# ScalarE makes the exponentials of a unit ahead of the copy of turned probabilities

## The chip, the cores and the metric

The kernel runs on one core of one Trainium2 chip. The metric is the device time of one launch in microseconds. Three runs of the kernel before took 4431.72 us in the median (4425.48 to 4433.78).

## The reference

The reference is one layer of a vision transformer over 64 images of 3 x 224 x 224, in fp32. It makes 196 patch tokens an image, adds two class tokens (198 tokens of width 192), applies attention and then a mixture of experts, each with a residual. The attention is what matters here:

```python
q, k, v = (qkv[0], qkv[1], qkv[2])                       # 12 heads of 64
attn = jnp.einsum('bhqd,bhkd->bhqk', q, k) * scale
attn = attn + jnp.einsum('bhqd,qkd->bhqk', q, r_p_k) * scale   # relative positions
attn = jax.nn.softmax(attn, axis=-1)
out = jnp.einsum('bhqk,bhkd->bhqd', attn, v)
out = out + jnp.einsum('bhqk,qkd->bhqd', attn, r_p_v)
out = out.transpose(0, 2, 1, 3).reshape(b, n, QKV_DIM)
return out @ proj_w.T + proj_b
```

## The kernel before

Three stages run one after the other: tokens (to about 465 us), attention (to about 3461 us), experts. The attention stage takes the images in 8 groups of 8. In a group there are 6 pairs of heads, and in a pair 16 units: one image and one head each, so 96 units (STEPS) in a group and 768 in all. A unit has 198 queries and 198 keys; both are handled in halves of 99.

Every engine runs through the same 96 steps of a group, and its instructions are written out in a fixed order. Semaphores tie the engines together. In step n:

- TensorE makes the scores of unit n (L1077), then turns the probabilities of unit n - 2 (four transposes, L1043) into one PSUM bank, the only one of its kind, then multiplies the turned probabilities of unit n - 3 with the values (L1060), and then does the step's jobs. Before it turns, it waits until POOL has normalised unit n - 2 and until ScalarE has copied the turned probabilities of unit n - 3 out of the bank (`probT_made`).
- VectorE takes the maxima of the scores (L870), inverts the sums of the unit before (L862), copies out the product of unit n - 3 (`put_out`, L854 and L855) and does its jobs.
- ScalarE copies the turned probabilities of unit n - 2 from PSUM (`turned_out`, L712), makes the exponentials of unit n (two ACTIVATEs at L724 with their sums) and does its jobs. The exponentials wait for the maxima (`peaks`), and for `turned`, since they write the buffer of probabilities that TensorE is turning (buffer i % 2).
- POOL multiplies the probabilities of a unit by the inverted sums (L631).

The jobs are the rest of the work, spread over the steps by a planner with a table of costs (`spread`): "first" jobs make queries (j below 4, copied by ScalarE at L686 to L689), keys (L692, L693), position terms (L697 on ScalarE, L814 on VectorE) and values (L703) of the next pair of heads; "last" jobs end the pair before (L822, L831 and L841 on VectorE, L1031 on TensorE). "turn" jobs make the normalised tokens of the next group: TensorE turns them (L991, L992), ScalarE copies them (L681, L682), VectorE makes the low part (L799, L800) and normalises the next ones (L780), and TensorE's projections (L998) need them. They lie at the end of a group. TensorE hands its results to the others through a ring of four PSUM banks. In two of the pairs of a group (p = 1 and p = 3) the planner's list has two query jobs behind each other, `f(K[0], Q[0], K[1], Q[1], Q[2], ...)`.

Once in each of the first seven groups, after step 72, ScalarE makes a square root for the next group's normalisation (L670, `deviation`). Square root and exponential lie in different tables, so an ACT_TABLE_LOAD stands before the square root and another before the next exponential.

Of the kernel before, what the change touches and what calls it, by code (L numbers as in the profile page):

```python
# [359 lines left out]
def attention_stage(nc, hidden0, qkv_w, proj_w, proj_b, tab_kv, tab_kh, tab_vv, tab_vh, hidden1):  # L360
# [16 lines left out]
    with ExitStack() as ctx:  # L377
# [152 lines left out]
        def base_of(g, v):  # L530

            return OPEN if v == "first" else g * G_JOBS + (OPEN + FIRST_JOBS - G_JOBS)
# [14 lines left out]
        with nc.Block() as block:  # L547
# [97 lines left out]
            def _(act):  # L645
                first = RAW // 2
# [22 lines left out]
                def deviation():  # L669
                    nc.scalar.activation(sd[:, :, :], mv[:, :, 1:2], ACT.Sqrt, bias=eps[0:HALF, :]).then_inc(sd_made, 1)  # L670
# [37 lines left out]
                def turned_out(n, i):  # L708
                    act.wait_ge(turned, n - 2 + 1)
                    if not isinstance(n, int) or n >= 4:  # L710
                        act.wait_ge(outs, n - 3)
                    nc.scalar.activation(probT[:, i % 2, :], t_bank[0:HALF, 0:2 * NTOK], ACT.Copy).then_inc(probT_made, 1)  # L712

                def group(g, s, v):
                    base = base_of(g, v)
                    for i in range(STEPS):
                        n = g * STEPS + i
                        if v != "first" or i >= 2:
                            turned_out(n, i)
                        act.wait_ge(peaks, n + 1)  # L720
                        if v != "first" or i >= 2:
                            act.wait_ge(turned, n - 1)
                        for h in range(2):
                            ins = nc.scalar.activation(prob[:, i % 2, h, :], s_bank[i % 2][0:HALF, h * NTOK:(h + 1) * NTOK],  # L724
                                                       ACT.Exp, bias=npeak[:, i % 2, h:h + 1],
                                                       accum_out=total[:, i % 2, h:h + 1])
                        ins.then_inc(exps, 1)
                        for j in spreads[v][i]:
                            job(base, g, v, *j)
                        if i == DEVIATION and v != "last":  # L730
                            act.wait_ge(mv_made, g + 2)
                            deviation()
# [10 lines left out]
                for j in opening[TURN:]:  # L743
                    job(0, 0, "opening", *j)
                groups(act, group)
                for i in range(STEPS, STEPS + 2):
                    turned_out((GROUPS - 1) * STEPS + i, i)
# [829 lines left out]
```

## Time and profile before

| what | value |
|---|---|
| median of three runs | 4431.72 us |
| the profiled execution | 4426.74 us |
| its span | 4425.0 us |
| mean granted TensorE clock | 0.963 |
| busy: TensorE, VectorE, ScalarE, POOL | 92%, 66%, 57%, 29% |
| copies of turned probabilities (L712) | 768 of 501 ns |
| exponentials (L724) | 1536 of 425 ns, and 1536 reads of their sums of 204 ns |

Busy time is the time in which an engine works on an instruction. An engine's idle time is put down to the instruction that ended it and to the engine that released that instruction. Successive instructions of ScalarE overlap: the next one can start before the row's time of the one before is over.

### The profile page before, as it was taken

To read this page: it belongs to the slowest core of one execution; us is meant where nothing else is said; L and a number is where in the kernel's file an instruction comes from. 1 tells how busy PE (TensorE), PEld (TensorE's weight loads), DVE (VectorE), ACT (ScalarE), POOL (GpSimd) and SP (SyncE) were. 2 spreads that over 40 slices of the span, in tenths; PEclk is the share of its full clock that TensorE was granted. 3 is DMA by queue.
4 is the path that set the end of the run, shared out by engine and by line. 5 is a ranking of instruction groups with operands and counts; after the bars stand their busy time and mean duration, and the time that the engine had idled before them with its cause. 6 is when DMAs were issued, how large, how long until landed. Compare 5 with 4: busy or idle time off the path is not lost. (4 is left out here: it accounts for less than half of the span.)

```text
span 4425.0 us, 84814 instructions
## 1 busy us (share of the span) xinstructions
PE 4084.1 (92%) x28203; PEld 3987.8 (90%) x28203; DVE 2922.1 (66%) x7468; ACT 2506.7 (57%) x6685; POOL 1273.7 (29%) x1423
## 2 busy tenths in 40 slices
PE   4986799899999999989989999999999799999999
PEld 4885699899899999989989998998999699999999
DVE  4675666666666766666666666666666577777776
ACT  2553666566666666656666666666665344444443
POOL 1232322222232222213222222221322244444443
PEclk8997899999999999999999999999999799999999
DMA  8543000000000000000000000000000222222222
GB/s 184 131 109 73 7 1 1 1 24 1 1 23 1 1 2 23 1 1 23 1 1 19 7 1 2 23 1 1 12 1 1 66 90 89 89 89 89 89 89 87
DMA packets 88973, 161.67 MB, mean 37 GB/s; under 512 B 5705, under 2 KB 75936, under 8 KB 85054
## 3 DMA queue, kind: packets, MB, share of 16 engines
q1 hardware_dynamic: 85118, 152.66, 12.1%
q0 software_dynamic: 944, 2.42, 0.3%
q8 instruction: 182, 2.98, 0.3%
q10 hardware_dynamic: 2576, 2.36, 0.2%
q14 instruction: 153, 1.25, 0.1%
HBM read 127.82 MB, written 29.60 MB: 36 GB/s over the span
## 5 line engine op out<-in xcount | busy, mean ns | idle before, releaser
L631 POOL TENSOR_TENSOR att_prob<-att_prob,att_total 99x396 f32<-99x396 f32 x768 | 650.9, 848 | 2279.0 <-DVE att_total L862 2279.0
L712 ACT ACTIVATE att_probT<-att_t 99x396 f32<-99x396 f32 x768 | 385.0, 501 | 737.4 <-PE att_t L1043 732.0
L870 DVE TENSOR_REDUCE att_npeak<-att_s 99x2 f32<-99x396 f32 x768 | 435.4, 567 | 451.7 <-PE att_s L1077 437.2
L724 ACT ACTIVATE att_prob<-att_s,att_npeak 99x198 f32<-99x198 f32 x1536 | 638.0, 425 | 80.3 <-DVE att_npeak L870 77.5
L1077 PE MATMUL att_s<-att_kx,att_qx 96*99 96x198 f32 (+1 forms) x3072 | 661.9, 339 | 4.5 <-DVE att_xres L841 2.3
L1060 PE MATMUL att_o<-att_probT,att_vx 99*96 99x198 f32 (+1 forms) x3072 | 663.1, 339 | 1.1 <-DVE att_rx L855 1.1
L1257 POOL TENSOR_TENSOR ffn_hidden<-ffn_relu 128x384 f32<-128x384 f32 x462 | 419.7, 914 | 494.8 <-ACT ffn_relu L1286 492.7
L1077 PEld LDWEIGHTS att_s<-att_kx,att_qx 96*99 96x99 f32 (+1 forms) x3072 | 494.3, 170 | 16.3 <-issue 5.3
L1286 ACT ACTIVATE ffn_relu<-ffn_h 128x384 f32<-128x384 f32 x462 | 226.3, 490 | 477.3 <-PE ffn_h L1503 476.5
L1515 PE MATMUL ffn_y<-ffn_down,ffn_hidden 128*128 128x192 f32 x2772 | 487.5, 326 | 0.0
L1060 PEld LDWEIGHTS att_o<-att_probT,att_vx 99*96 99x96 f32 (+1 forms) x3072 | 477.2, 181 | 5.8 <-issue 1.4
L1515 PEld LDWEIGHTS ffn_y<-ffn_down,ffn_hidden 128*128 128x128 f32 x2772 | 457.8, 190 | 1.2 <-issue 0.2
L854 DVE COPY att_oT<-att_o 64x198 f32<-64x198 f32 x768 | 277.1, 361 | 240.7 <-PE att_o L1060 233.2
L1043 PEld LDWEIGHTS att_t<-att_ident,att_prob 99*99 99x99 f32 x3072 | 396.1, 170 | 37.5 <-issue 21.9
L1043 PE MATMUL att_t<-att_ident,att_prob 99*99 99x99 f32 x3072 | 405.0, 255 | 20.3 <-ACT att_probT L712 16.5
L855 DVE COPY att_rx<-att_o 32x198 f32<-32x198 f32 x768 | 404.1, 526 | 10.4
L1408 DVE TENSOR_TENSOR ffn_hidden<-ffn_hidden,ffn_gates 64x384 f32<-64x384 f32 (+1 forms) x528 | 362.4, 702 | 20.5 <-issue 3.8
L1031 PE MATMUL att_p<-att_pw,att_oT 128*99 128x192 f32 x1536 | 292.6, 334 | 80.9 <-DVE att_oT L831 80.9
L1031 PEld LDWEIGHTS att_p<-att_pw,att_oT 128*99 128x99 f32 x1536 | 247.7, 169 | 89.6 <-issue 88.1
L724 ACT ACTIVATION_READ_ACCUMULATOR att_prob<-att_s,att_npeak 99x1 f32 x1536 | 313.3, 204 | 0.0
L814 DVE TENSOR_TENSOR att_qx<-att_p,att_qx 32x448 f32<-32x448 f32 (+1 forms) x384 | 226.4, 590 | 63.7 <-PE att_p L1008 35.4
L348 PE MATMUL tok_y<-tok_w,tok_patchT 128*112 128x192 f32 x1344 | 249.6, 339 | 10.5 <-DVE tok_y L282 10.5
(237 smaller groups left out, 8170.7 us busy)
## 6 DMA issues: line engine op xcount, KB each, us to landing
ffn_gates<-gate_rows SPq DMA_DIRECT2D x66, 768.0 KB, 5.0
tok_pixels<-in_x SPq DMA_DIRECT2D x24, 1568.0 KB
ffn_hid<-hidden SPq DMA_DIRECT2D x35, 288.0 KB, 3.0
att_xres<-hidden SPq DMA_DIRECT2D x8, 1188.0 KB
hidden<-att_xres SPq DMA_DIRECT2D x8, 1188.0 KB
ffn_acc<-hidden SPq DMA_DIRECT2D x33, 288.0 KB, 2.9
out_hidden<-ffn_acc SPq DMA_DIRECT2D x33, 288.0 KB, 2.4
hidden<-tok_rows SPq DMA_DIRECT2D x7, 1176.0 KB
```

The source lines that it names most:

```text
L631: nc.gpsimd.tensor_tensor(prob[:, i % 2, :, :], prob[:, i % 2, :, :], view(total[:, i % 2, :], [[1, 2], [0, NTOK]]), ALU.mult).then_inc(pr ...
L712: nc.scalar.activation(probT[:, i % 2, :], t_bank[0:HALF, 0:2 * NTOK], ACT.Copy).then_inc(probT_made, 1)
L724: ins = nc.scalar.activation(prob[:, i % 2, h, :], s_bank[i % 2][0:HALF, h * NTOK:(h + 1) * NTOK], ACT.Exp, bias=npeak[:, i % 2, h:h + 1], ...
L855: nc.vector.tensor_copy(view(rx[ext:ext + 32, p % 2, :], [[GB, NTOK]], b), o_bank[ext:ext + 32, 0:NTOK]).then_inc(outs_used, 1)
L870: nc.vector.tensor_reduce(npeak[:, i % 2, :], s_bank[i % 2][0:HALF, 0:2 * NTOK].rearrange("p (h k) -> p h k", h=2), AX.X, ALU.max, negate= ...
L1031: ins = nc.tensor.matmul(bank[0:HALF, t * DIM:(t + 1) * DIM], oT[:, s, cols], pw[:, weights, :], start=True, stop=True)
L1043: ins = nc.tensor.transpose(t_bank[0:HALF, k * NTOK + h * HALF:k * NTOK + (h + 1) * HALF], prob[:, j % 2, h, k * HALF:(k + 1) * HALF], ide ...
L1060: ins = nc.tensor.matmul(o_bank[0:M, 0:NTOK], vx[:, 2 * b + k, p % 2, v0:v0 + M], probT[:, j % 2, k * NTOK:(k + 1) * NTOK], start=(k == 0) ...
L1077: ins = nc.tensor.matmul(s_bank[i % 2][0:HALF, h * NTOK:(h + 1) * NTOK], qx[0:K, p % 2, head, q0:q0 + HALF], kx[0:K, p % 2, head, b * NTOK ...
L1257: nc.gpsimd.tensor_tensor(hidden[0:rows, s, j, :], relu[0:rows, (n + 2 * s) % 4, :], relu[0:rows, (n + 2 * s) % 4, :], ALU.mult).then_inc( ...
L1408: ins = nc.vector.tensor_tensor(hidden[lo:hi, s, j, :], hidden[lo:hi, s, j, :], gates[lo:hi, s, e, :], ALU.mult)
L1515: ins = nc.tensor.matmul(y_bank[t][:, 0:DIM], hidden[:, s, j, t * 128:(t + 1) * 128], down[:, j, :], start=(n == 0), stop=(n == HT - 1))
```

## The change

In the loop over the steps ScalarE calls `turned_out` behind the two exponentials and no longer ahead of their waits. The waits of the exponentials stay as they are. The two calls behind the last group, and the other engines' programs, are unchanged.

```diff
@@ -715,8 +715,6 @@
                     base = base_of(g, v)
                     for i in range(STEPS):
                         n = g * STEPS + i
-                        if v != "first" or i >= 2:
-                            turned_out(n, i)
                         act.wait_ge(peaks, n + 1)
                         if v != "first" or i >= 2:
                             act.wait_ge(turned, n - 1)
@@ -725,6 +723,8 @@
                                                        ACT.Exp, bias=npeak[:, i % 2, h:h + 1],
                                                        accum_out=total[:, i % 2, h:h + 1])
                         ins.then_inc(exps, 1)
+                        if v != "first" or i >= 2:
+                            turned_out(n, i)
                         for j in spreads[v][i]:
                             job(base, g, v, *j)
                         if i == DEVIATION and v != "last":
```

## Rows read from the trace of the kernel before

**Rows 1.** The page, part 1: busy us (share of the span) xinstructions.
```profile
PE 4084.1 (92%) x28203; PEld 3987.8 (90%) x28203; DVE 2922.1 (66%) x7468; ACT 2506.7 (57%) x6685; POOL 1273.7 (29%) x1423
```

**Rows 2.** TensorE's waits, 560 to 3465 us: total us, times, longest us.
```profile
PE att_p L1031 <- DVE att_oT L831: 80.2, 47, 2.3
PE att_p L998 <- DVE att_x L800: 31.1, 7, 4.4
...
PE att_t L1043 <- ACT att_probT L712: 15.0, 16, 1.0
PE att_t L1043 <- POOL att_prob L631: 3.7, 5, 0.8
```

**Rows 3.** Groups by line: busy, mean ns of one | idle before, releaser.
```profile
L712 ACT ACTIVATE att_probT<-att_t 99x396 f32<-99x396 f32 x768 | 385.0, 501 | 737.4 <-PE att_t L1043 732.0
...
L724 ACT ACTIVATE att_prob<-att_s,att_npeak 99x198 f32<-99x198 f32 x1536 | 638.0, 425 | 80.3 <-DVE att_npeak L870 77.5
```

**Rows 4.** Timeline of one step: start us, duration us, engine, line, [idle before].
```profile
3413.38 0.51 PE L1043 MATMUL att_t<-att_ident,att_prob 99*99 99x99 f32 x4
3413.59 0.57 DVE L870 TENSOR_REDUCE att_npeak<-att_s 99x2 f32<-99x396 f32 x1
...
3413.93 0.50 ACT L712 ACTIVATE att_probT<-att_t 99x396 f32<-99x396 f32 x1 [1.68 <-PE att_t L1043]
...
3414.33 0.42 ACT L724 ACTIVATE att_prob<-att_s,att_npeak 99x198 f32<-99x198 f32 x1
...
3415.21 0.59 PE L1043 MATMUL att_t<-att_ident,att_prob 99*99 99x99 f32 x4
```

**Rows 5.** Timeline, 937 to 942 us, behind two query jobs.
```profile
937.33 0.50 ACT L712 ACTIVATE att_probT<-att_t 99x396 f32<-99x396 f32 x1
...
938.04 0.51 PE L1043 MATMUL att_t<-att_ident,att_prob 99*99 99x99 f32 x4
...
941.30 0.50 ACT L712 ACTIVATE att_probT<-att_t 99x396 f32<-99x396 f32 x1
...
941.95 0.56 PE L1043 MATMUL att_t<-att_ident,att_prob 99*99 99x99 f32 x4 [0.95 <-ACT att_probT L712]
```

**Rows 6.** Timeline, 1514 to 1525 us, behind the square root.
```profile
1514.95 0.50 ACT L712 ACTIVATE att_probT<-att_t 99x396 f32<-99x396 f32 x1
...
1515.47 1.28 ACT L724 ACT_TABLE_LOAD   x1
...
1516.11 0.51 PE L1043 MATMUL att_t<-att_ident,att_prob 99*99 99x99 f32 x4
...
1516.46 0.86 PE L1060 MATMUL att_o<-att_probT,att_vx 99*128 99x198 f32 x4
...
1516.77 0.43 ACT L724 ACTIVATE att_prob<-att_s,att_npeak 99x198 f32<-99x198 f32 x1
...
1517.92 0.37 DVE L854 COPY att_oT<-att_o 64x198 f32<-64x198 f32 x1
...
1524.32 0.86 PE L1031 MATMUL att_p<-att_pw,att_oT 128*99 128x192 f32 x4 [2.29 <-DVE att_oT L831]
```

**Rows 7.** Timeline, 1547 to 1550 us, at the next group's tokens.
```profile
1547.58 0.43 ACT L724 ACTIVATE att_prob<-att_s,att_npeak 99x198 f32<-99x198 f32 x1 [0.56 <-DVE att_npeak L870]
...
1548.40 0.33 ACT L681 ACTIVATE att_x0h<-att_p 128x198 fp32r<-128x198 f32 x1
...
1549.81 0.67 PE L998 MATMUL att_p<-att_x0h,att_w0h 128*128 128x396 f32 x1 [4.44 <-DVE att_x L800]
```

**Rows 8.** ScalarE's waits, 1530 to 1572 us.
```profile
ACT att_prob L724 <- DVE att_npeak L870: 5.3, 7, 1.5
```

**Rows 9.** VectorE's waits, 560 to 3465 us.
```profile
DVE att_oT L854 <- PE att_o L1060: 228.5, 554, 1.4
...
DVE att_total L862 <- ACT att_prob L724: 17.0, 23, 1.1
```

**Rows 10.** Windows: span, busy us of PE, PEld, DVE, ACT, POOL, PEclk, DMA share, GB/s.
```profile
1524.30:1527.90 3.60, 3.58 (x18) 3.50 (x19) 1.28 (x4) 1.32 (x5) 0.85 (x1) 0.72 0.00 0
```

## The prediction

> **What bounds the kernel now.** I read the page first: TensorE is busy 92% of the span, ScalarE 57%, so time comes only from TensorE's idle stretches and whatever fills them [rows 1]. The diff touches the attention stage only (768 units in 8 groups of 96, about 490 to 3461 us of the span, so 3.9 us a unit), so the next view is what TensorE waits for there: 47 waits for VectorE's adds (L831), 7 long ones where the next group's tokens are turned (L998 behind L800), and 16 waits of 15.0 us in all for the turned probabilities' copy (L712) [rows 2]. That copy is what the change moves back. ScalarE itself idles 737 us in front of that copy and 80 us in front of the exponentials [rows 3]. So its work is spare on average; the question is where it is not.
>
> **What the edit does to an ordinary step.** Of the two waits that now precede the exponentials, one is no wait for a new thing: the exponentials of unit n overwrite the probabilities that TensorE is just turning (buffer i % 2), and the code keeps its wait on `turned`. So they can't start before the transposes end, change or no change. An ordinary step shows the size of it [rows 4]: transposes end at 3413.38 + 0.51 = 3413.89, copy at 3413.93, exponentials at 3414.33; VectorE's reduction ends at 3413.59 + 0.57 = 3414.16. New order: exponentials at about 3414.20, only 0.13 us earlier. The pair holds ScalarE for 0.82 us (worked out from rows at place 3); the copy then starts at 3415.02 instead of 3413.93 and ends at 3415.52. A copy holds ScalarE 0.40 us before the next instruction starts [rows 4], and TensorE restarts 0.15 us after a copy that it waits for (941.30 + 0.50 = 941.80, restart 941.95 [rows 5]). So TensorE's next transposes could start at 3415.67. A step of this stage is 3.9 us on average, transposes to transposes, and here 3413.38 + 3.9 = 3417.3: the delay lies free in nearly every step. The gain lies free as well: POOL and VectorE get the exponentials 0.13 us earlier, and TensorE's waits for POOL are 3.7 us in all [rows 2]. No instruction, byte or DMA is added or removed; SP's and POOL's queues aren't passed.
>
> The rule by which I look for losses: the copy is late by the exponentials' 0.8 us where ScalarE comes late anyway (it no longer goes first), and by more where the maxima are late; a ScalarE job behind both is late by the copy's 0.40 us where the copy was formerly hidden in the wait for the maxima.
>
> **Place 1, the heads' projections (16 times).** Twice in each group two query jobs follow each other, and ScalarE falls behind. Its copy of 937.33 comes 2.3 us after the transposes; TensorE turns on at 938.04; the next copy is at 941.30 and TensorE has waited 0.95 us for it at 941.95 [rows 5]. New: the first copy starts at 937.33 + 0.82 = 938.15, ends 938.65, TensorE goes on at 938.80, 0.76 us late. That alone is then absorbed by the 0.95 us wait. But the second copy also starts 0.82 us later, at 942.12, and TensorE goes on at 942.77 instead of 941.95: 0.82 us. The pair of steps costs 0.82, not the sum. There is one such wait for each of the 16 counted [rows 2]. Nothing later swallows it: VectorE, who makes the later waits at L831, itself waits for TensorE in between (554 waits at L854 [rows 9]), so it moves along. 16 x 0.82 = 13.1 us. Bounds: 0 (all absorbed) and 16 x 1.58 = 25 (no absorption between the two); I take 13.1, as the rows in sequence give it.
>
> **Place 2, after the deviation (7 times).** ScalarE has taken a square root and must load the exponentials' table again, 1.28 us. Before, the copy (1514.95) came ahead of the load (1515.47) [rows 6]. New: load 1514.95 to 1516.23, exponentials to 1517.05, copy ends 1517.57, TensorE's transposes start at 1517.72 instead of 1516.11: 1.6 us. What is late next is VectorE: it needed the product of 1516.46 + 0.86 = 1517.32 but came to it only at 1517.92; 1.6 us later, at 1518.92, it is 1.0 us behind. VectorE then works without a pause up to the adds that TensorE waits for at 1524.32 (2.29 us wait [rows 6]), so 0.6 of the 1.6 us vanish in that wait and 1.0 remains. 7 x 1.0 = 7.0 us (bounds 0 and 11).
> On this the Trainium skill has a rule that speaks against the change: "ScalarE: Activation LUTs", section "What ACT_TABLE_LOAD costs", gives a switch of the table set 1283 ns for the load and about 1380 ns more for a drain, some 2.66 us. By it the moved load would weigh 1.38 us more, 7 x 1.4 = 10 us on top. The row shows a load of 1.28 us with the exponentials 0.02 us behind it (1515.47 + 1.28 = 1516.75, then 1516.77 [rows 6]), so the trace gives no such drain here and the sum goes without it.
>
> **Place 3, where the next group's tokens are turned (7 times).** Here the three engines hand each other work and TensorE is the one that waits. ScalarE has made its copy, waits 0.56 us for the maxima, makes the exponentials at 1547.58 and, 0.82 us later, copies the turned tokens at 1548.40; VectorE's subtraction L800 follows; TensorE, idle for 4.44 us, goes on at 1549.81 [rows 7]. VectorE was late with the maxima, so the copy had been free; now it stands between exponentials and tokens, and the whole chain is 0.40 us later. The stretch of 42 us has 7 such waits for the maxima [rows 8]. I followed each: behind five of them a query or token job lies on this chain (the first three add up to the restart at 1549.81, one leads to TensorE's next restart near 1559.5, one to that near 1568), 5 x 0.40 = 2.0; and once ScalarE, late at 1553.6, must now wait 0.2 us for maxima. 2.2 us a group, 7 x 2.2 = 15.4 us. Bounds: 0, and 7 x 7 x 0.40 = 20. An early loss of 0.4 us on TensorE's side of the same stretch is hidden by the 4.44 us wait.
>
> **Last group.** Five steps without jobs: TensorE's next transposes at 3415.67 instead of 3415.21, [rows 4], 0.45 us, then an estimated 0.2 us a step, since from there on VectorE, held up by 0.45 us with its maxima, passes part of it on: about 1.5 us.
>
> **Sum.** 13.1 + 7.0 + 15.4 + 1.5 = 37 us. The profiled execution took 4426.7 us (span 4425.0), 5.0 below the median 4431.7 of three: 4463.7 on its scale, 4468.7 on the median's. I say 4466.
>
> **The clock.** TensorE's granted clock falls to its lower level, 1.2 GHz, after some of its waits: after the 2.29 us wait that ended at 1524.32 [rows 6] the next 3.6 us are granted 0.72 [rows 10], so the fall costs 3.6 x 0.28 = 1.0 us. After the 0.95 us wait it didn't: those transposes take 0.56 us, the ones before 0.51 [rows 5]. The new waits, 0.8 to 1.4 us, lie nearer to this one. I count no fall.
>
> **Rivals**, from 4429, which lies between the two times as 4466 does.
> Clock: the lengthened waits at places 1 and 2 (23) pull it down each time: 23 x 1.0 = 23 us more, 4489. For it: place 1 has two waits of 0.8 and 1.0 us within 4 us. Against: the 0.95 us wait cost nothing.
> Absorption: TensorE's losses at places 1 and 2 disappear in the 80 us of waits for L831, as 0.6 of 1.6 us does after the deviation; places 3 and the end remain: 4429 + 17 = 4446. Against: VectorE waits for TensorE more often than the reverse.
> Faster: exponentials no longer behind the copy. VectorE's reciprocals waited 23 times, 17.0 us, for them [rows 9], most where ScalarE is late; each comes 0.40 us earlier, 9 us, and the 3.7 us of waits for POOL go: 4429 - 13 = 4416. It decides if these reciprocals stand at the head of VectorE's chain to TensorE, rather than ahead of a wait for TensorE's product as at L854. I see them ahead of that wait.
> Nothing: two operations trade places inside ScalarE's 737 us of idle time and the late steps are too few: 4429. For it are the ordinary steps; against it the 16 waits where the copy is already what TensorE lacks.
>
> **How the numbers follow.** Forecast 64% (its own range 4452 to 4480: each place by a third either way), clock 12%, absorption 12%, faster 6%, nothing 6%. The range, 4440 to 4498, leaves out the two last and takes in the clock case with a third more; a change under 0.2% (9 us) can't be told from none here. Faster 0.06, same 0.08 (nothing, and the low end of absorption), slower 0.86.
>
> **What would show it.** TensorE's waits for the copy (L712) go from 16 with 15.0 us to about 45 with some 45 us, 1.4 us at each table load; the wait for L800 from 4.4 to about 5.2 us; ScalarE's idle time moves from in front of the copy to in front of the exponentials; the load at L724 stands ahead of the copy. Busy times stay. It is wrong if TensorE's waits for L712 stay near 15 us, if those at L831 shrink by as much as L712's grow, or if the mean granted clock changes by over 0.005.

## The result, and the profile after

| | before | after |
|---|---|---|
| median (20 runs each) | 4432.16 us | 4441.33 us |
| lowest to highest | 4416.45 to 4439.62 us | 4435.71 to 4446.98 us |
| profiled execution, its span | 4426.74, 4425.0 us | 4446.40, 4444.7 us |
| mean granted clock in it | 0.963 | 0.964 |

The ratio is 1.0025, 95% interval 1.0017 to 1.0033: slower by about 9 to 11 us, where 37 were forecast. The profiled executions stand 20 us apart; the one of before lies 5 us below its median and the one of after 5 us above.

TensorE's waits of the profile after, 560 to 3480 us (total us, times, longest us); against [rows 2] the copy's go from 15.0 to 38.3 us, those at L831 fall by 3.7, those for L800 grow by 4.2, and the wait for POOL is as good as gone.

```profile
PE att_p L1031 <- DVE att_oT L831: 76.5, 47, 1.8
PE att_t L1043 <- ACT att_probT L712: 38.3, 52, 1.4
PE att_p L998 <- DVE att_x L800: 35.3, 7, 5.1
PE att_p L998 <- issue: 21.3, 14, 2.3
...
PE att_t L1043 <- POOL att_prob L631: 0.2, 1, 0.2
```

ScalarE's groups after (busy, mean ns of one, idle before). Its idle time has moved from in front of the copy [rows 3] to in front of the exponentials, now L722, as forecast.

```profile
L722 ACT ACTIVATE att_prob<-att_s,att_npeak 99x198 f32<-99x198 f32 x1536 | 640.6, 422 | 931.6 <-DVE att_npeak L870 869.5 <-PE att_t L1043 58.7
L712 ACT ACTIVATE att_probT<-att_t 99x396 f32<-99x396 f32 x768 | 382.6, 498 | 1.8 <-PE att_t L1043 1.8
```

The timeline at place 1, the steps of [rows 5]. ScalarE is late at 947.70 and makes exponentials; the copy follows 0.82 us later and TensorE waits 0.57, then 0.96 us.

```profile
947.70 0.43 ACT L722 ACTIVATE att_prob<-att_s,att_npeak 99x198 f32<-99x198 f32 x1
...
948.52 0.50 ACT L712 ACTIVATE att_probT<-att_t 99x396 f32<-99x396 f32 x1
...
949.16 0.56 PE L1043 MATMUL att_t<-att_ident,att_prob 99*99 99x99 f32 x4 [0.57 <-ACT att_probT L712]
...
953.13 0.56 PE L1043 MATMUL att_t<-att_ident,att_prob 99*99 99x99 f32 x4 [0.96 <-ACT att_probT L712]
```

The timeline at place 2, the steps of [rows 6]: load, exponentials, copy, then TensorE; the wait at L1031 that follows is 1.75 instead of 2.29 us.

```profile
1528.21 1.28 ACT L722 ACT_TABLE_LOAD   x1
1529.51 0.43 ACT L722 ACTIVATE att_prob<-att_s,att_npeak 99x198 f32<-99x198 f32 x1
...
1530.33 0.50 ACT L712 ACTIVATE att_probT<-att_t 99x396 f32<-99x396 f32 x1
...
1530.97 0.56 PE L1043 MATMUL att_t<-att_ident,att_prob 99*99 99x99 f32 x4 [1.42 <-ACT att_probT L712]
...
1538.68 0.86 PE L1031 MATMUL att_p<-att_pw,att_oT 128*99 128x192 f32 x4 [1.75 <-DVE att_oT L831]
```

The timeline at place 3, the steps of [rows 7]: from the exponentials at 1561.03 to the tokens at 1562.23 it is now 1.20 us instead of 0.82, and TensorE waits 5.05 instead of 4.44 us.

```profile
1561.03 0.43 ACT L722 ACTIVATE att_prob<-att_s,att_npeak 99x198 f32<-99x198 f32 x1 [1.09 <-DVE att_npeak L870]
...
1561.85 0.50 ACT L712 ACTIVATE att_probT<-att_t 99x396 f32<-99x396 f32 x1
1562.23 0.34 ACT L681 ACTIVATE att_x0h<-att_p 128x198 fp32r<-128x198 f32 x1
...
1563.64 0.67 PE L998 MATMUL att_p<-att_x0h,att_w0h 128*128 128x396 f32 x1 [5.05 <-DVE att_x L800]
```

The longest of the new waits for the copy lies ahead of the 560 us from which the waits above are counted, at step 3 of the first group; the same wait was 1.31 us before, at 517.65.

```profile
519.39 0.56 PE L1043 MATMUL att_t<-att_ident,att_prob 99*99 99x99 f32 x4 [2.12 <-ACT att_probT L712]
```

**Step by step.** The start of each unit's scores (L1077) in both profiles gives the length of each of the 768 steps. Of the 96 steps of a group, those listed differ, and steps 82 to 86, where both kinds of difference mix; the others agree to 0.05 us but for a few at the start of group 0 and where two groups meet. (Differences after minus before, us, by group 0 to 7. Step 19 is the one from the scores of unit 19 to those of unit 20. The starts are read to 0.01 us, so a difference can be off by 0.02.)

```
step 19        0.77  0.79  0.78  0.78  0.78  0.75  0.77  0.77
step 51        0.78  0.78  0.78  0.77  0.78  0.75  0.79  0.78
step 74        1.64  1.63  1.63  1.63  1.64  1.65  1.64   -
step 75       -0.55 -0.56 -0.54 -0.54 -0.55 -0.56 -0.57   -
step 79        0.42  0.41  0.41  0.40  0.41  0.41  0.41   -
step 81        0.74  0.72  0.73  0.74  0.75  0.73  0.75  0.33
steps 12, 13   0.29 -0.01  1.66  0.04 -1.68  0.03 -0.01 -1.68
steps 28, 29   1.67  0.00 -0.01  0.00 -1.66 -1.67 -1.66 -1.66
step 45        0.02 -1.66 -1.65  1.66  0.00  0.00  0.00  0.01
steps 60, 61   1.68  0.01  0.01  0.00 -1.65 -1.67  0.03 -1.66
step 76       -0.01 -1.66 -1.67  1.67  0.01  0.00  1.67  0.01
```

The upper rows are the three places, the same in each group. The lower ones are 0 or 1.66 us of either sign: something that comes or doesn't. The windows of step 60 show what it is (columns as in [rows 10]; 4 us from the end of a wait for L831 that is 1.56 us long each time). Before, groups 2 and 3:

```profile
1466.80:1470.80 4.00, 4.00 (x28) 3.95 (x29) 2.59 (x8) 1.32 (x5) 0.85 (x1) 1.00 0.02 4
1839.80:1843.80 4.00, 4.00 (x16) 3.70 (x17) 1.29 (x4) 0.50 (x2) 0.45 (x1) 0.57 0.00 0
```

After, the same groups:

```profile
1480.00:1484.00 4.00, 3.95 (x28) 3.93 (x29) 2.52 (x7) 1.31 (x5) 0.84 (x1) 1.00 0.00 0
1858.20:1862.20 4.00, 4.00 (x16) 3.66 (x17) 1.29 (x4) 0.77 (x4) 0.77 (x1) 0.57 0.00 0
```

The same 1.56 us wait is followed once by the full clock, 28 products in 4 us, once by a fall to 1.2 GHz, 0.57 and 16 products. A fall costs TensorE 1.66 us there. Behind the waits of 1.56 to 1.76 us at steps 12, 28, 44 and 60 there are 16 falls in before and 9 in after: 7 x 1.66 = 11.6 us given back. (A fall is counted for a wait when the granted clock goes down in it or in the 3 us behind it.)

**The clock in all executions.** Two profiles alone wouldn't show that the falls are fewer. But the mean granted clock is on record for 87 executions of the kernel before (0.960 to 0.965, mean 0.9626) and for 31 of the kernel after (0.964 to 0.967, mean 0.9657). The profiled executions of before had 0.963 and 0.964 (experiment 1), above their mean, those of after 0.964 and 0.965 (experiment 6), below theirs.

### The profile page after: what moved, and what is told of

Its sections match the earlier page's. It is cut to its first block and busy times, and to the rows that moved or that the text cites. A ratio compares the mean times of both kernels' runs of the same rounds, so it can differ in the third digit from the quotient of the medians.

```text
span 4444.7 us, 84808 instructions
## 1 busy us (share of the span) xinstructions
PE 4083.2 (92%) x28203; PEld 3982.7 (90%) x28203; DVE 2919.8 (66%) x7468; ACT 2482.2 (56%) x6685; POOL 1271.8 (29%) x1423
## 5 line engine op out<-in xcount | busy, mean ns | idle before, releaser
L722 ACT ACTIVATE att_prob<-att_s,att_npeak 99x198 f32<-99x198 f32 x1536 | 640.6, 422 | 931.6 <-DVE att_npeak L870 869.5
L1077 PE MATMUL att_s<-att_kx,att_qx 96*99 96x198 f32 (+1 forms) x3072 | 658.0, 337 | 4.8 <-DVE att_xres L841 2.7
L1077 PEld LDWEIGHTS att_s<-att_kx,att_qx 96*99 96x99 f32 (+1 forms) x3072 | 490.7, 169 | 15.7 <-issue 5.6
L712 ACT ACTIVATE att_probT<-att_t 99x396 f32<-99x396 f32 x768 | 382.6, 498 | 1.8 <-PE att_t L1043 1.8
L1031 PE MATMUL att_p<-att_pw,att_oT 128*99 128x192 f32 x1536 | 292.2, 333 | 77.2 <-DVE att_oT L831 77.2
L1031 PEld LDWEIGHTS att_p<-att_pw,att_oT 128*99 128x99 f32 x1536 | 248.6, 169 | 86.1 <-issue 84.4
L722 ACT ACTIVATION_READ_ACCUMULATOR att_prob<-att_s,att_npeak 99x1 f32 x1536 | 301.7, 196 | 0.0
L348 PE MATMUL tok_y<-tok_w,tok_patchT 128*112 128x192 f32 x1344 | 250.1, 339 | 11.6 <-DVE tok_y L282 11.6
```

Source lines behind the costliest of these rows:

```text
L1031: ins = nc.tensor.matmul(bank[0:HALF, t * DIM:(t + 1) * DIM], oT[:, s, cols], pw[:, weights, :], start=True, stop=True)
L1077: ins = nc.tensor.matmul(s_bank[i % 2][0:HALF, h * NTOK:(h + 1) * NTOK], qx[0:K, p % 2, head, q0:q0 + HALF], kx[0:K, p % 2, head, b * NTOK ...
```

## The experiments

Each kernel was compared with the kernel before on the same chip. The median of before differs a little from one comparison to the next (4430.41 us for experiments 1 to 4, 4428.03 for 5 to 8, 4432.62 for 9 to 12), so kernels of different comparisons are to be held against each other by their ratios.

**1. The kernel before against itself.** No edit.

> The kernel before, unchanged, against itself. It leaves nothing out. Theory 'lottery of the clock': the waits of 1.4 to 2.3 us for the adds at L831 and L800 lie at the edge of a fall of the granted clock, a fall costs 1.66 us, and how many there are (33 stretches at the low level in the attention stage of the profiled execution) differs from one execution to the next. Then this profile shows another number of low stretches, another pattern of them, and a span of the attention stage that differs from 2942.9 us (first to last scores) by 3 to 10 us, while steps with no fall take the same time to 0.1 us. Rival 'the profile of before was typical': the same stage to within 1 us, and the change costs its 18 us there in every execution. The medians agree within 0.1% under both.

Measured: 4430.42 us (11 runs), before 4430.41 (33), ratio 1.0000 (0.9989 to 1.0010). From first to last scores 2946.5 us, 2942.5 in the other profile. The two profiles of one kernel differ by plus or minus 1.66 us at steps 12 and 13, 28 and 29, 44 and 45, 60 and 61, and 76, by up to 2.4 us at 82 to 86, and nowhere else by more than 0.2 us beyond the first group's first 20 steps and one place where two groups meet. There are 32 stretches at the low clock in the attention stage, 33 in the other profile. Step 60 in this profile, groups 1 and 2, where the first profile had the full clock:

```profile
1098.40:1102.40 4.00, 4.00 (x16) 3.66 (x17) 1.29 (x4) 0.54 (x2) 0.48 (x1) 0.57 0.00 0
1473.90:1477.90 4.00, 4.00 (x16) 3.70 (x17) 1.29 (x4) 0.47 (x2) 0.42 (x1) 0.57 0.02 4
```

So falls come and go between executions of one kernel; single profiles can't be compared by span. Their number at the four steps is 18 here.

**2 to 5. Places undone one by one.** The kernel after with the old order in some steps:

```diff
+    COPY_FIRST = (73,)                 # 2: behind the square root
+    COPY_FIRST = (18, 19, 50, 51)      # 3: behind the query jobs
+    COPY_FIRST = tuple(range(78, 86))  # 4: the tokens
+    COPY_FIRST = (18, 19, 50, 51, 73, *range(78, 86))  # 5: all three
...
+                        if i in COPY_FIRST and (v != "first" or i >= 2):
+                            turned_out(n, i)
                         act.wait_ge(peaks, n + 1)
...
-                        if v != "first" or i >= 2:
+                        if i not in COPY_FIRST and (v != "first" or i >= 2):
                             turned_out(n, i)
```

> The kernel after, with the old order (copy first) in one step of 96, the one behind the square root (step 73). Theory 'places': TensorE's waits for the copy lose their 7 longest (1.4 us each, 38.3 us in 52 becomes about 28 in 45), the step of 1.64 us at 75 of each group and the -0.55 behind it vanish, the kernel is 7.6 us faster than after, that is 0 to 0.1% above before (4432 + 9 - 8 = 4433 to 4437). Rival 'absorbed': the 2.29 us wait for L831 that follows takes its 1.64 us back wholly, time as after (4441).

> The kernel after, with the old order in the four steps of 96 where ScalarE is behind with query jobs (18, 19, 50, 51). Theory 'places': the 16 losses of 0.78 us vanish (12.5 us): as before or faster, 4429 to 4433; TensorE's waits for the copy fall from 38.3 us in 52 to about 22 in 36. Rival 'absorbed later': time as after (4441), since the waits at L831 grow by as much.

> The kernel after, with the old order in the eight steps of 96 where the next group's tokens are turned (78 to 85). Theory 'places': the wait for L800 is 4.4 us again instead of 5.1, and 2.1 us a group vanish, 15 us in all if my sum was right: 4427. Rival, from the two profiles (2.1 us a group in groups 0 to 2, about 0 in groups 3 to 6, where both have long stretches at the low clock): 5 to 7 us, 4435. If this place costs nothing in the median, time as after.

> The kernel after, with the old order in all three places (13 of 96 steps: 18, 19, 50, 51, 73, 78 to 85), the new order in the other 83. Theory 'places': no wait for the copy is left but the 16 of 0.95 us that were there before; time as before, 4430, within 0.1%. Rival 'the new order is itself worth something in the ordinary steps', for which speaks that the rest of the stage was 7 to 16 us shorter with it in four profiles: 4418 to 4424. Rival 'it costs in the ordinary steps too': 4435 and more.

| kernel | median us (runs) | ratio to before (interval) | waits for the copy, us (times) | falls at steps 12, 28, 44, 60; at the L831 wait of step 75 | mean clock of all executions |
|---|---|---|---|---|---|
| after | 4441.33 (20) | 1.0025 (1.0017 to 1.0033) | 38.3 (52) | 9; 3 | 0.9657 |
| 2, table | 4438.35 (11) | 1.0015 (1.0005 to 1.0025) | 28.0 (45) | 10; 2 | 0.9652 |
| 3, late | 4435.69 (11) | 1.0011 (1.0002 to 1.0020) | 29.0 (37) | 10; 6 | 0.9635 |
| 4, tokens | 4432.53 (11) | 1.0008 (0.9999 to 1.0017) | 34.3 (40) | 7; 4 | 0.9665 |
| 5, all three | 4432.29 (11) | 1.0010 (1.0000 to 1.0020) | 14.9 (17) | 18; 2 | 0.9618 |

For the kernel before the last two columns are 16; 3 and, in experiment 1, 18; 0, and 0.9626.

Kernels 2 and 3 came out 1 and 3 us above what was expected, kernel 4 5.5 us above the theory's 4427 and 2.5 under the rival's 4435. Each place is confirmed by its waits: 10.3 us go with the table's, 9.3 with the queries' (16 were expected), the 5.05 us wait for L800 becomes 4.4 again in kernel 4. Their gains (by the ratios 4, 6 and 8 us, against 7.6, 12.4 and 14.3 us of direct delay) are hardly above the intervals' plus or minus 4 us. They don't behave as a sum: with all three undone the kernel is no better than with the third alone. The waits of kernel 5 are those of before [rows 2]:

```profile
PE att_p L1034 <- DVE att_oT L834: 80.4, 47, 2.3
PE att_p L1001 <- DVE att_x L803: 31.0, 7, 4.4
...
PE att_t L1046 <- ACT att_probT L713: 14.9, 17, 0.9
```

and so is its number of falls, 18, though 83 of its 96 steps have the new order. With one place undone they are 7 to 10.

**6. The kernel after once more.** No edit.

> The kernel after, unchanged, once more. The 8 steps named for each group are slower by the same amounts to 0.05 us (0.78, 0.78, 1.64 with -0.55 behind it, 0.41, 0.74), and the falls of the clock behind the waits of 1.56 to 1.76 us stand elsewhere and number about 9 again, not the 16 and 18 of the two profiles of before. If they number 16 or more, their smaller number was chance.

Measured: 4439.83 us (11 runs), before 4428.03 (27), ratio 1.0027 (1.0018 to 1.0036). Falls at the four steps: 9 again, 7 of them at the same step of the same group as in the first profile of after. Waits for the copy 38.0 us in 52, and the steps named are the same to 0.03 us. The smaller number isn't chance: the mean clock is 0.9656 in these 11 executions and 0.9629 in the 27 of before beside them. It goes with the delays: 16 and 18 falls without them, 18 in kernel 5, which has hardly any, 7 to 10 with two or three of the three places. Kernel 3, with 6 falls more at step 75 and a mean clock of 0.9635, lies nearest to before.

**7 and 8. The clock taken out of play.** TensorE makes products of no use (fillers) in its long waits, in the order before (7) and after (8):

```diff
+                def fill(k, base, count):
+                    pe.wait_ge(free[k % RING], base + k // RING + PRIMED)
+                    for _ in range(count):
+                        nc.tensor.matmul(p_bank[k % RING][:, 0:384], ident[:, :], view(ident[:, :], [[0, 3], [1, 128]]),
+                                         start=True, stop=True)
...
+                    if v != "opening" and kind == "first" and j < 4 and p == NEXT:
+                        fill(k, base, (0, 11, 3, 1)[j])
...
                     if kind == "last" and j == 8:
+                        fill(k, base, 3)
                         all_read(base, v, "last", p, 7, other)
```

> The kernel before, in which TensorE no longer sits idle in its long waits: ahead of the waits for L831 it makes 3 products of the identity with itself (N = 384) in the free bank that its own job overwrites, and where the tokens are turned 11, 3 and 1. Nothing is left out. Theory 'the clock decides': the 32 or 33 low stretches of the attention stage go to under 12, each 1.6 us, and the kernel gains 25 to 35 us: 4395 to 4407. Rival 'the products only take time': they delay the restarts, 47 times some tenths of a us, and nothing is gained: 4430 to 4445.

> The kernel after with the same fillers. Theory 'the order costs 28 us, and fewer falls of the clock give 10 to 18 of them back': with the falls gone in both kernels, this one is 22 to 28 us above f1 (12.4 for the heads' projections, 7.6 at the table load, 2 to 8 at the tokens): about 4425. Rival 'the order costs 9 us': f2 stands 9 us above f1.

Measured: 7, 4400.14 us (5 runs), ratio 0.9939 (0.9925 to 0.9952), no fall in the attention stage: 'the clock decides' (4395 to 4407) held, and the 5 executions lie within 4.2 us of each other, where those of the kernel before spread over 23. 8, 4433.95 us (11 runs), ratio 1.0012 (1.0003 to 1.0021), 4 falls (two behind the 1.42 us waits for the copy, one behind the 2.11 us wait for it at step 3, one at step 16 of the first group). Between them 33.8 us, where the plain kernels differ by 9 to 12. Step by step the losses of the plain kernels stand there again (0.77 us at 19 and 51, 1.63 less 0.53, 0.41), only step 81 loses 0.33 instead of 0.74. The waits for the copy are the ones we know, in 7 and then in 8:

```profile
PE att_t L1052 <- ACT att_probT L712: 14.4, 16, 0.9
```

```profile
PE att_t L1052 <- ACT att_probT L712: 46.5, 59, 1.4
```

The rival for 8 (9 us) is out, and my 22 to 28 was too low.

**9. Only the moment moved.** The kernel before, TensorE busy 0.87 us longer twice a group:

```diff
+                    if kind == "last" and p in (0, 2) and j == 2:
+                        for n in (3 * 128, 64):
+                            nc.tensor.matmul(bank[:, 0:n], ident[:, :], view(ident[:, :], [[0, max(n // 128, 1)], [1, min(n, 128)]]),
+                                             start=True, stop=True)
```

> The kernel before, old order, in which TensorE works 0.76 us more twice in a group (products of the identity, N = 384 and 64, in the bank of the job that follows, at the heads' pairs where the new order costs 0.78 us). Nothing is left out. Theory 'the moment decides': which of the waits of 1.6 us is followed by a fall depends on when they come, and a group of 372 us repeats the falls. Then this delay alone lowers the falls behind the waits at steps 12, 28, 44 and 60 from 16 to 18 to about 9, and gives back its own 12 us: 4425 to 4434. Rival 'the new order itself protects the clock': the falls stay at 16 to 18 and the kernel is 12 us slower, 4442.

Measured: 4436.82 us (11 runs), before 4432.62 (16), ratio 1.0004 (0.9992 to 1.0017). The steps 22 and 54 are longer by 0.87 us in all 8 groups, 13.9 us, and the kernel by 2 to 4 us. Falls at the four steps: 11, and 3 at step 75. Mean clock of its 11 executions 0.9647, of the 16 of before 0.9626. The waits themselves are those of before:

```profile
PE att_p L1035 <- DVE att_oT L831: 80.2, 47, 2.3
PE att_p L1002 <- DVE att_x L800: 31.0, 7, 4.4
...
PE att_t L1047 <- ACT att_probT L712: 14.3, 16, 0.9
```

A delay alone, the order untouched, lowers the falls and gives a part of itself back: 10 to 12 of the 13.9 us by the medians and the ratio, at least 6 by the interval. The rival (4442, the order itself protects the clock) is out: 12 us would be a ratio of 1.0027. The median came 3 us above my interval's upper end of 4434. The delay here is work of TensorE, in kernels 2 to 4 it is waiting; the falls are fewer with both.

**10 to 12. Fillers made to size, and the ordinary steps.** In 10 (order before) and 11 (order after) the counts are 2 ahead of L831's waits and 6, 2 and 0 at the tokens; 12 is kernel 5 with the fillers of 7.

```diff
-                        fill(k, base, (0, 11, 3, 1)[j])
+                        fill(k, base, (0, 6, 2, 0)[j])
...
-                        fill(k, base, 3)
+                        fill(k, base, 2)
```

> The kernel before with fillers made to size: one product of N = 384 took 0.65 us, so three of them (1.95 us) were longer than the waits of 1.5 to 1.76 us, and eleven (7.2 us) longer than 4.44. Now 2 ahead of L831's waits, and 6, 2 and 0 at the tokens. Theory: no falls still, and 0.1 to 0.25 us saved at 47 places and up to 1.6 us at 7: 4388 to 4396. Rival: the 0.3 to 1 us of idle time that comes back lets the clock fall again: 4400 to 4410.

> The kernel after with the fillers of g2. Theory 'the order costs its sum once the clock is out of play': 30 to 37 us above g2. Rival 'some of f2 minus f1 came from the oversized fillers': under 25 us.

> The kernel after with the old order in the three places (13 of 96 steps), and the first, oversized fillers of f1. Theory 'the ordinary steps are free': f1 plus the 3.2 us that the first group's start costs (steps 3 to 16), 4400 to 4405. Rival 'the new order costs or saves in the 83 other steps': off by more than 5 us from f1.

Measured: 10, 4384.66 us (4 runs), ratio 0.9891 (0.9875 to 0.9906), the fastest of all, 3 us under the 4388 to 4396 expected. 11, 4418.52 us (7 runs), 0.9969 (0.9957 to 0.9980): 33.9 us above 10, inside the 30 to 37. 12, 4402.43 us (5 runs), 0.9935 (0.9921 to 0.9949), inside the 4400 to 4405: 2.3 us above 7, the ratios equal to 0.0004, and step by step only the first group's steps 3 to 14 differ, by 1.2 us in all. So the other 83 steps are free, as the timeline had shown. The waits of 10, then of 11:

```profile
PE att_p L1007 <- issue: 20.5, 21, 1.4
PE att_p L1040 <- DVE att_oT L831: 19.5, 46, 1.0
...
PE att_t L1052 <- ACT att_probT L712: 14.8, 16, 0.9
PE att_t L1052 <- POOL att_prob L631: 6.0, 8, 0.8
```

```profile
PE att_t L1052 <- ACT att_probT L712: 47.0, 59, 1.4
PE att_p L1007 <- issue: 26.0, 21, 1.8
PE att_p L1040 <- DVE att_oT L831: 15.5, 46, 0.5
...
PE att_t L1052 <- POOL att_prob L631: 0.2, 1, 0.2
```

Falls in the attention stage are 5 and 4, none at the four steps; 4 of those of kernel 10 lie at step 85, behind a wait of 0.77 us for POOL.

## Why the prediction was right or wrong

**The sum of direct delays was right to 3 us.** The kernel became 9 to 12 us slower. That is far under the 37 forecast, and 4441.33 lies below the forecast's own 4452 to 4480; that it is just inside the wider 4440 to 4498 is luck, since that low end was made for losses absorbed in the waits at L831. The sum itself said 37 us; with all but a few of the falls gone the two orders differ by 33.8 and 33.9 us. Its terms, by the step table (and for steps 83 and 85 of place 3 by kernels 7 and 8):

| term | predicted us | measured us |
|---|---|---|
| place 1, 16 times | 13.1 (0.82 each) | 12.4 (0.78 each) |
| place 2, 7 times | 7.0 (1.6 less 0.6) | 7.6 (1.64 less 0.55) |
| place 3, 7 times | 15.4 (2.2 each) | 13.3 (0.41 + 0.74, and 0.38 + 0.37 in kernels 7 and 8) |
| last group | 1.5 | 1.0 |
| start of the first group | not seen | 1.2 (a fall behind the 2.12 us wait in it) |

Place 3 was over-sized by one link: the steps give 0.41, 0.74, 0.38 and 0.37 us where I had counted five times 0.40 and once 0.2. At the start of the stage ScalarE is late as well, in steps 3 to 14 of group 0 alone; I had read no row there. That nothing absorbs the delays at place 1, that 0.6 us vanish behind place 2, and that the ordinary steps cost nothing, held. So did the choice of the row over the page on the table load: behind the 1.28 us load at 1528.21 the exponentials start at 1529.51, 0.02 us later, so there is none of the 1380 ns drain that "ScalarE: Activation LUTs" of the Trainium skill adds in its section "What ACT_TABLE_LOAD costs".

**The step that failed is "The clock ... I count no fall".** I asked whether the new waits would bring falls, and they hardly do: none behind the 0.57 and 0.96 us waits at place 1, none in either profile of after behind the 1.42 us waits at the table load, one behind the 2.12 us wait of step 3, where I had read no row. I didn't ask what becomes of the falls that the kernel before already has. It has 33 in the attention stage of its profile, half of them behind waits of 1.6 us that are followed by a fall in one group and not in the next. My price was wrong as well. It came from one row [rows 10], 1.0 us for the 2.29 us wait, but that window ends at 1527.90 while the low clock lasts to about 1529.3:

```profile
1525.80:1529.30 3.50, 3.50 (x17) 3.32 (x16) 2.15 (x7) 1.32 (x5) 0.85 (x1) 0.51 0.00 0
```

The whole fall costs 1.66 us. With the change the falls at the four steps go from 16 and 18 down to 9: 7 to 9 times 1.66, 12 to 15 us back. At place 3 a part comes back too: in both profiles of before step 85 holds a 0.77 us wait for POOL (4 and 6 of 7 groups) and falls behind it (4 of 7 each time); in both of after there is neither. The stretch of steps 78 to 88 of the first seven groups took 350.5 and 354.0 us before and 357.2 and 357.1 after, 4.9 more on average instead of 13.3: 8 us back. So 36 of direct delays less 13 and less 8 leave 15 us; the four profiles show 16 on average for the stage (2942.5 and 2946.5 before, 2960.6 and 2959.9 after). The medians show 9 to 12. The rest fits which executions were profiled: both of after lay 5 us above their medians and below their mean clock.

**The signs on record didn't catch this.** The waits for the copy grew (38.3 us in 52 where 45 in 45 were forecast, 1.42 us at each load), the wait for L800 became 5.05 us, the idle time moved, and the load stands first, all much as forecast. And none of the signs of being wrong appeared: the waits at L831 fell by 3.7 us against the copy's 23.3 more, and the mean clock moved by 0.001 in the profiles and 0.003 over all executions, where the sign asked for 0.005. These signs tested the direct delays. By an estimate from the 1.66 us that a fall costs, 0.005 of 4430 us is some 13 falls and 0.003 some 8.

**The rivals.** Absorption gave 4446, nearest to the result, by the wrong mechanism: it let place 1 vanish in the waits for L831, while those 0.78 us are whole in every group. "Clock" had the sign reversed. "Faster" had one true piece, the waits for POOL (5 waits, 3.7 us, then 0.2), which went. "Nothing", 4429, is out: the interval of the ratio begins at 1.0017.

**What stays open.** That a shift of the moment is enough to change the number of falls is shown by experiment 9. Why the groups of the kernel before (371.9 to 377.0 us from group 1 on, falls included) are struck more often than those of after (373.1 to 380.6) is not. In both profiles of before the falls of a step come in runs of groups (step 60: five in a row, then all eight); in the first profile of after those of steps 60 and 75 come in groups 0, 3 and 6 and those of steps 28 and 44 in groups 0 and 3, in the second the same but for group 5 in the place of 6. That looks like a repetition in step, but no run varied the length of a group finely enough to show it. That a new order would keep its 9 falls in another kernel can't be concluded.

## What to carry to other kernels

Take the delays link by link from the timeline where the engine comes late, not from its average idle time: that sum was good to 3 us. Then count the falls of the clock that the kernel before already has, above all those behind waits that are followed by a fall only sometimes; any shift of time can change their number. Here that gave back 20 to 25 of 36 us; no shift was tried that cost more than it did directly. Without any shift the executions of the kernel before spread over 23 us. A median over many executions, the mean clock of all of them and a second profile are needed to see it. Where such waits stand, products of no use in a bank that is free anyway, as long as the wait and no longer, are worth more than the order of two instructions: 1.09% here.

## What the runs showed of the hardware

- The granted clock after a wait of one length isn't determined by that length: 1.62 us at step 28 was followed by a fall in 5 and 4 of 8 groups in the kernel before, in 5 in kernel 5, in 2 and 2 with the new order and in 1 in experiment 9, old order. The 1.50 us wait at step 93 never was, in 63 cases of the nine profiles without fillers, while that at step 60, about 1.56 us in groups 0 to 6, was in 3 to 7 of these 7.
- A fall costs 1.66 us at the adds' steps. At the tokens, where TensorE waits for VectorE, falls cost as well: all 7 waits of 4.44 us had one in the kernel before; in kernel 10 these are gone (4 falls at step 85 stay), and steps 78 to 88 took 367.3 us in all groups, against 379.1 and 382.6, some 2 us a group.
- An fp32 product of the identity, 128 x 128 with N = 384, took TensorE 0.65 us and stands as two records in the trace; so my first fillers, three of 0.65 us, were longer than the waits of 1.5 to 1.76 us. Made to size they gained another 15.5 us by the medians (4400.14 to 4384.66) and 21 by the ratios (0.9939 to 0.9891).
